# Order of VectorE's work at the end of the second attention: tile 0's weighted sums in one piece, tile 4's search ahead of the last row groups' normalisation

## The reference, cut to what is computed

```python
# third layer: graph attention on the normalised rows
scores = where(adj > 0, leaky_relu(s1[:, None] + s2[None, :], 0.2), NEG)
x = x + elu(softmax(scores) @ (layernorm(x) @ W))
# fourth layer: product keys, per head
xn = layernorm(x)
sim = (xn @ Wq_pk) against 2 x 128 keys        # two halves of 128 scores each
top 16 of each half -> 256 sums -> top 16 of those, with their row numbers
k, v = softmax(best 16) weighted sums of 16 rows of keys_table and values_table
out = causal attention(q = xn @ Wq, k, v) @ Wo
x = x + sum over heads of out
```

## Time and profile before

| | |
|---|---|
| median of three runs | 2866.45 us (2860.98 to 2868.05) |
| span of the profiled execution | 2859.2 us; no total time of its own is given for it, the three runs lie 1.8 to 8.9 us above it |
| VectorE busy | 2373.7 us, 83% |
| GpSimd busy | 1959.6 us, 69% |
| TensorE matmul busy | 1591.0 us, 56% |
| ScalarE busy | 744.9 us, 26% |
| first gather starts | 254.42 us |
| last gather starts | 2836.43 us |

### The profile page before, as it was taken

One profiled execution on the slowest core, in us unless ns is written; L12 is line 12 of the kernel. 1 busy time (PEld: TensorE's weight loads), 2 busy tenths in 40 slices (PEclk: granted clock), 3 DMA queues, 4 the chain that ended last, 5 costly groups with the idle time before them and its releaser, 6 DMA issues. The chain is left out here.

```text
span 2859.2 us, 31735 instructions
## 1 busy us (share of the span) xinstructions
PE 1591.0 (56%) x7362; PEld 1220.4 (43%) x7362; DVE 2373.7 (83%) x8263; ACT 744.9 (26%) x1904; POOL 1959.6 (69%) x2064
## 2 busy tenths in 40 slices
PE   6858545664556445554556455554555445554555
PEld 6848434453344334442344234442344333442444
DVE  6689899998888888887888888887888888887874
ACT  5746412231122112221122112221122112221212
POOL 0003777777777777777777777777777777777775
PEclk8969756785578557775677557775678557775678
DMA  4201233333333333333333333333333333333333
GB/s 158 102 1 34 86 103 105 109 107 105 105 108 106 107 105 108 105 106 106 106 108 106 106 105 108 105 107 105 105 108 106 107 105 108 105 107 106 106 105 90
DMA packets 109551, 291.44 MB, mean 102 GB/s; under 512 B 34128, under 2 KB 41808, under 8 KB 107344
## 3 DMA queue, kind: packets, MB, share of 16 engines
q0 software_dynamic: 98304, 268.57, 32.1%
q1 hardware_dynamic: 10080, 20.97, 2.1%
q10 hardware_dynamic: 1008, 0.33, 0.0%
HBM read 288.69 MB, written 1.05 MB: 101 GB/s over the span
## 5 line engine op out<-in xcount | busy, mean ns | idle before, releaser
L288 POOL DMA_INDIRECT ring<-table,rows x2048 | 1952.1, 953 | 714.4 <-issue 587.9
L755 DVE SCALAR_TENSOR_TENSOR ps<-ring,wgt,ps 128x256 f32<-128x256 f32 x1792 | 865.6, 483 | 316.7 <-DMA ring<-table,rows 290.2
L1608 PE MATMUL ps<-ident,work 128*128 128x128 f32 x1088 | 260.2, 399 | 526.7 <-PEq L1601 526.7
L1608 PEld LDWEIGHTS ps<-ident,work 128*128 128x128 f32 x1088 | 201.4, 211 | 581.9 <-issue 581.8
L1622 PE MATMUL ps<-s2w,work 128*128 128x128 f32 x2176 | 418.7, 358 | 35.2 <-PEq L1620 34.4
L1622 PEld LDWEIGHTS ps<-s2w,work 128*128 128x128 f32 x2176 | 381.0, 265 | 84.5 <-issue 82.0
L1590 PE MATMUL ps<-work,qT 128*128 128x512 f32 (+3 forms) x576 | 310.7, 680 | 69.3 <-PEq L1582 64.8
L1296 ACT ACTIVATE s2w<-ps 128x512 f32<-128x512 f32 (+2 forms) x320 | 168.7, 533 | 332.2 <-ACTq L1295 331.8
L1286 ACT ACTIVATE work<-ps,nmax 128x128 f32<-128x128 f32 (+15 forms) x128 | 149.3, 1167 | 318.7 <-ACTq L1284 318.7
L1577 PE MATMUL ps<-ident,work 128*128 128x128 f32 x128 | 46.8, 366 | 316.9 <-PEq L1575 316.9
L1590 PEld LDWEIGHTS ps<-work,qT 128*128 128x128 f32 x576 | 124.9, 238 | 200.0 <-issue 200.0
(11 more groups left out here) (241 smaller groups left out, 2654.3 us busy)
## 6 DMA issues: line engine op xcount, KB each, us to landing
ring<-table,rows POOLq DMA_INDIRECT x2048, 2.7
staged<-adj_in SPq DMA_DIRECT2D x16, 1024.0 KB, 4.8
xs<-x_in SPq DMA_DIRECT2D x4, 256.0 KB, 6.3
wpkq<-w_pkq SPq DMA_DIRECT2D x8, 128.0 KB
out<-xs SPq DMA_DIRECT2D x1, 832.0 KB, 4.4
keyd<-pk_keys SPq DMA_DIRECT2D x16, 32.0 KB
wo<-w_o SPq DMA_DIRECT2D x8, 64.0 KB
out<-xs SPq DMA_DIRECT2D x1, 192.0 KB, 2.1
```

The costliest lines, as they stand in the source:

```text
L288: nc.gpsimd.indirect_dma_start(ring[:, t % RING, k, :], None, table_d, bass.IndirectOffsetOnAxis(ap=rows[:, t % RING, k:k + 1], axis=0),). ...
L755: return v.scalar_tensor_tensor(out, row, w, acc_ps, ALU.mult, ALU.add)
L1608: ins = m.transpose(ps[:, 2 + (parity + b) % 2, j % 4 * P:(j % 4 + 1) * P], prob[:, t % 2, j * P:(j + 1) * P], ident[:, :])
```

## The change

Only the order of calls in VectorE's program changes. Both halves of tile 0's sums now stand right behind `find_all(3)`. The first half of tile 4's search follows them, then `elu_out(3)`, then the second half. `normal(3)`, `elu_in(4)`, `weigh(2)`, `elu_out(4)` and `normal(4)` keep their order among themselves and come behind all of it. No instruction is added or removed, and the programs of the other engines are the same.

```diff
             find_all(3)
+            sum_half(0, 0)
+            sum_half(0, 1)
+            find_halves(4)
             elu_out(3)
-            sum_half(0, 0)
+            find_all(4)
             normal(3)
             elu_in(4)
             weigh(2)
             elu_out(4)
-            sum_half(0, 1)
             normal(4)
             rows_done(1)
-            find_halves(4)
-            find_all(4)
             settle()
             dve.sem_inc(dve_done, -c.n)
             c.n = 0
             weigh(AHEAD - 1)
             settle()
             for t in range(1, T):
                 step(0, t, True, False)
```

## The result

The changed kernel takes 2870.64 us (median of 21 runs, 2869.55 to 2875.1) against 2866.45 us before (21 runs, 2860.98 to 2868.14). The ratio is 1.0016, with a 95% interval of 1.0010 to 1.0022: about 4.2 us longer, 2.9 to 6.3 us by the interval. That is small, within 0.3%, but clear of no change. The forecast was 2871.5 us, +5.0 us.

A forecast was written before the change was run, and what follows sets the result against it. The prediction took GpSimd's chain of gathers as the bound: -6.13 us for the gap removed at tile 4 and +11.13 for the new one at tile 5 made +5.0, so 2866.45 became 2871.5 us, range 2863 to 2877.

The forecast's parts named there:

- What bounds the kernel: GpSimd's gathers, about 1.25 us each from start to start, set the end; VectorE leads tile 5's gather by only 1.38 us.
- The fixed tail: After the last gather's start the kernel takes a constant time, so the end follows the sum of GpSimd's real gaps.
- Sums of tile 0: On VectorE, both halves in one piece, started at 326.90, end at 335.4 us with no wait for rows.
- Tile 4's search and gather: With `elu_out(3)` inside the search, the cast starts at 347.6 and GpSimd's gather at 351.20, a gain of 6.13 us.
- The last two groups: Row groups 3 and 4 lose their cover on VectorE; `step(0, 1)` starts at 363.3, a lag of 6.3 us.
- Tile 5's gather: Its cast starts at 381.2 and the gather at 382.3 against 377.33, 5.0 us later, with a GpSimd gap of 11 us.
- Behind it: From tile 6 on VectorE is ahead by 3.8 us and more, so the 5.0 us shift stays to the end.
- The sum: GpSimd's removed gap, -6.13 us, and the new one, +11.13 us, make +5.0 us, or 2871.5 us.
- GpSimd did not stay fed: Rival: tile 4's gather starts 6.13 us earlier and nothing is given back, 2860.3 us; chance 0.05.
- the answers did not come in time: Rival: ScalarE or TensorE answers faster, so VectorE's lag is small; 2865.1 us with no lag; chance 0.09.
- VectorE was not the bound: Rival claimed VectorE is the bound and its lag goes through in full, +6.3 us, 2872.8 us; chance 0.10.
- the wait at `step(0, 2)` did not come: Rival claimed VectorE waits 3.6 us for similarities again at that step, +8.6 us, 2875.1 us; chance 0.04.

The follow-up runs named there:

- the sums alone: Kernel before with both halves of tile 0's sums ahead of `elu_out(3)`, tile 4's search left at the end: 2863.33 us against 2861.91.
- the search alone: Kernel before with tile 4's search ahead of the normalisation, second half of the sums left before `normal(4)`: 2866.15 us against 2861.91.
- the projection first: Changed kernel with tile 5's projection and tile 3's exponential ahead of row groups 3 and 4 on TensorE and ScalarE: 2863.25 us against 2861.91 before.
- work under each answer: Same calls as the kernel before, reordered with one piece of sums or search under each answer: 2858.79 us against 2861.91.
- late by one operation: Kernel before with one extra 1.09 us VectorE operation between `weigh(3)` and `step(0, 1)`: 2860.62 us against 2861.16.
- late by six: Kernel before with six extra VectorE operations, 6.5 us, between `weigh(3)` and `step(0, 1)`: 2867.55 us against 2861.16.
- groups between the steps: Changed kernel with row groups 3 and 4 finished between head 0's steps on VectorE, ScalarE and TensorE: 2860.43 us against 2866.08 before.

## Why the prediction was right

- **What bounds the kernel.** Right. GpSimd's chain of gathers is the bound. Shown, from tile 4 on, by 6.5 us of added work on VectorE that cost nothing at step 12, and by each kernel's time following the start of tile 5's gather:

  | | expected there, us | in the trace | in the time |
  |---|---|---|---|
  | the sums alone | +1.3 | +1.3 | +1.4 |
  | the search alone | +4.1 | +4.3 | +4.2 |
  | the projection first | +1.5 | +1.3 | +1.3 |
  | work under each answer | -3.6 | -2.9 | -3.1 |
  | late by one operation | 0.0 | +0.1 | -0.5 |
  | late by six | +5.1 | +5.2 | +6.4 |
  | groups between the steps | -6.1 | -6.4 | -5.7 |

- **The fixed tail.** Fixed only roughly: from the last gather's start to the end of the span it takes 21.6 to 23.9 us in the profiles, and differs by 0.5 us between the two profiles of the changed kernel. The prediction gave it no spread; it is one more reason to take shifts from medians of many runs and not from two spans.
- **Sums of tile 0.** Forecast to end at 335.4; they ended at 334.80 + 0.48 = 335.28 and the search began at 335.63, behind 0.35 us of waiting at L673 (0.17 in the earlier trace rows), where the prediction had no new wait. The date hides a little luck. VectorE was already some 0.4 us early in this execution before the changed order began (the gap before tile 2's gather is 1.12 us and not 1.55), so the sums began at 326.53 and not at 326.90; they took 8.75 us and not 8.47.
- **Tile 4's search and gather.** Cast at 347.6 forecast, 347.77 measured; gather at 351.20 forecast, 351.31 measured. From the start of the sums to the cast 20.64 us were forecast and 21.24 measured: the 0.6 us too little and the early start nearly cancel. Why the wait of 0.35 us arose is open.
- **The last two groups.** `elu_in(4)` at 348.7 (348.81), `elu_out(4)` at 353.1 (353.21), `normal(4)` at 355.8 (355.89), the step at 363.3 (363.44). The durations of the chains of answers, taken from where they had been hidden, held to 0.1 us. That the last of them is only a place in two queues was argued in the prediction and is shown by the run that moved the projection.
- **Tile 5's gather.** 382.3 forecast, 382.20 measured, with 11.4 us of idle time forecast before it and 10.99 measured. Counted from the start of the sums, which is free of the early start, this gather was forecast after 55.4 us and came after 55.67 in the first profile of the change and 55.66 in the second, against 50.43 in the profile before: the change's own shift is 5.2 us in both.
- **Behind it.** No further gap; tile 6's cast at 397.40 (397.4 forecast).
- **The sum.** +5.0 us forecast; +4.2 us in the first comparison (2.9 to 6.3) and +5.0 us in the second (2.3 to 7.5).
- **The weak step.** The prediction carried its shift from one profile over to the median, 7.25 us above the profiled span, without asking what those 7.25 us were. Some 2 us are what every run reads above its span; the rest is that the profile before fits the shortest execution, 5.5 us below the median. The longer pitch, seen in the profile after, would make 4.8 us of it, but no profile of a longer execution of the kernel before shows that. Carrying the shift over as a difference was right all the same.
- **The skill's rule.** The Trainium skill, Perfetto Trace Analysis, Identifying the Most-Contended Engine, names the engine with the highest occupancy. The runs here do not agree: VectorE has 83% and GpSimd 69% in both profiles, and 6.5 us more work on VectorE cost nothing where its lead was 35 us, and 6.4 us (3.4 to 8.6) where its lead was 1.38 us.
- **The rivals.** GpSimd did not stay fed; the answers did not come in time; VectorE was not the bound; the wait at `step(0, 2)` did not come.

## What to carry to other kernels

When one engine's chain of issues sets the end, judge a reordering by the date of each item's release against the date at which that engine could take it, for several items and not only for the one with the gap: a gap that is closed at one item can open wider at the next, where the lead was small. Work that lies under another engine's answers is cover; before moving it forward, write down which answer it leaves bare and how long that answer takes. And look at where the late work is first needed: what stood here in the path at tile 5 was not needed before tile 10, and finishing it in steps with slack was worth more (-5.7 us) than the best order of the old pieces that was tried (-3.1 us).

## What the runs showed of the hardware that was not expected

The pitch of the indirect DMAs issued by GpSimd was 1.2501 to 1.2505 us in eight profiles (the kernel before and the seven kernels on the first two chips) and 1.2526 us in three (the changed kernel twice, once of them on the third chip, and the groups between the steps on that chip), with median durations of 946 ns in the profile before and 949 ns in these three. It is even along the span and does not follow the order of work. Whether it goes with the chip or with the execution stays open. Over 2000 gathers it is 5 us, as much as the change under study, so kernels of this kind are to be compared side by side on one chip and over many executions, and two single profiles can differ by it.
